# First attention: both kinds of score products issued together over four row groups, output product ahead of the weighing; second mixture: row numbers read behind the third result

## The chip, the core and the metric

One core of one Trainium2 chip runs the whole program in one launch. The time is the device time in microseconds (us) from launch to end; the kernel before has a median of 1166.97 us over 3 runs (1165.14 to 1170.62). The engines named below are TensorE (PE: matrix products; its weight loads are shown as PEld), VectorE (DVE), ScalarE (ACT), GpSimd (POOL) and SyncE (SP), which here only starts DMAs. The engines run side by side, each in its own fixed order, and wait for each other on semaphores that are written out by hand.

## The reference, cut to what matters

Two layers, each an attention and a mixture of experts, over 16 sequences of 128 tokens with 256 features. The change touches the first attention and the last mixture.

```
# first attention: 16 heads of 16, per sequence
qh, kh, vh = split_heads(norm(x) @ Wq + bq), split_heads(ctx @ Wk + bk), split_heads(ctx @ Wv + bv)
attn = softmax(qh @ kh.T / sqrt(16))
x = x + tanh(g) * ((attn @ vh) @ Wo + bo)

# second mixture: 8 experts, each takes its 640 best (token, weight) pairs
kept_w, kept_pair = top_k(where(assigned, pair_w, -inf), 640)
xe = xf[kept_tok]
oe = gelu(xe @ fc1_w.T + fc1_b) @ fc2_w.T + fc2_b
y = zeros.at[kept_tok].add(oe * kept_w)
```

## The kernel before, in words

**First attention (`attention_0`).** A step `t` handles one sequence in several stages at once, a software pipeline over t = -3 to 18; sequence i is normed at step i-3, turned at i-2, projected to queries, keys and values at i-1, scored at i, exponentiated at i+1, weighed with the values at i+2, and multiplied with the output weights at i+3. Beside this, each step turns one half of an expert's weight matrix for the first mixture to signs (18 halves: `below` on POOL, `signs` and `magnitudes` on DVE, `turn_half` on PE, `keep` on ACT); after every odd half the row scales are spread over the partitions (`spread` on PE, then `keep_scale` on ACT, which comes behind `exps(i, 1)` in ACT's order).

The 16 heads sit in four row groups r = 0 to 3 of 32 partitions, four heads in each. Scores are made twice. `scores(i, ph)` makes them with queries as rows (`psS`, 4 products 32 rows deep and 256 columns wide for the row groups 2ph and 2ph+1), only so that DVE can take each row's maximum (`maximum(i, ph)`). `turn_maxima` turns these maxima, ACT copies them, and `less_maxima(i, ph)` makes the scores again with keys as rows (`psT`, 8 products of 32 x 128), and subtracts the maxima with 8 small products of 8 rows (`sel` against `nmT`). ACT then exponentiates `psT` (`exps`), and `weigh` multiplies with the values on PE in four column groups of 32 columns at once. `heads_out` on DVE divides by the sums, `output` on PE multiplies with Wo into one half of the bank `psV`, and `residual` on DVE adds to x. Every fp32 product shows up in a trace as two MATMUL records, so "x8" of `psS` in a timeline is one call of `scores`, and "x16" of `psT` and "x8" of `sel` one call of `less_maxima`.

Both halves ph share two banks of `psS` and two of `psT`. So `scores(i, 1)` waits for `maximum(i, 0)`, and `scores(i+1, 0)` for `maximum(i, 1)` (semaphore `max_done`); likewise `less_maxima` for `exps` (`exp_done`). PE's order in a step: scores(t,0), turn_maxima(t-1), value and project(t+1), less_maxima(t-1,0), scores(t,1), turn_in(t+2), weigh(t-2), turn_half(t), less_maxima(t-1,1), spread(t) if t is odd, output(t-3). DVE's: maximum(t,0), values, normed, maximum(t,1), split, heads_out(t-2), signs, magnitudes, residual(t-3), statistics.

**Second mixture (`feed_forward_1`).** After routing, the tokens are scattered in the order of experts to DRAM (`m_sorted`), with each row's destination in an extra column. Each expert e has 640 rows, NT = 5 tiles of 128. SP loads an expert's rows to `xin[e % 2]` (`load_x`; the name in the trace is `m_turned`), PE turns them, makes the hidden layer (`xup`) and the result (`xdown`), DVE adds the bias into one of NY = 4 buffers (`put`, tile `f_y`), and POOL scatters that buffer to its destinations (`send`, `m_results<-f_y,f_index`). POOL learns the destinations with `read_index(e)`, which waits for the load of `xin[e % 2]`. Expert 0's results are all made before expert 1's tiles are turned (`SECOND`), while the later experts are interleaved (`TURNS`). The fifth result of expert 0 needs the first buffer back, so `put(0, 4)` waits for `send(0, 0)` to land; the turned tiles of expert 1 stand behind it on DVE, and PE waits for those.

Of the kernel before, what the change touches and what calls it, by code (L numbers as in the profile page):

```python
# [138 lines left out]
def attention_0(nc, A, sb, ps, sem, NB, D, KD, x_sb, ctx_sb, ident, gates, x_mean, x_rstd, c_mean, c_rstd,  # L139
# [8 lines left out]
    NG = 4  # L148
    NQK, NV = 3, 4
# [4 lines left out]
    with ExitStack() as c:  # L154
# [7 lines left out]
        sel = sb("a0_sel", [P, NG, P], F32R, c)  # L162
# [54 lines left out]
        def there(i):  # L217
            return 0 <= i < NB

        with nc.Block() as block:  # L220
# [175 lines left out]
            def _(dve):  # L396
# [105 lines left out]
                def step(t):  # L502
# [8 lines left out]
                    if there(t):  # L511
                        maximum(t, 1)
                        split(t)
                    if there(t - 2):
                        heads_out(t - 2)
# [4 lines left out]
                    if there(t - 3):  # L520
                        residual(t - 3)
# [10 lines left out]
            def _(pe):  # L532
# [35 lines left out]
                def scores(i, ph):  # L568
                    b = i % NQK
                    if ph == 0:  # L570
                        pe.wait_ge(s["qk_out"], i + 1)
                    at_least(pe, s["max_done"], 2 * i + ph)
                    for m in range(2):
                        for r in (2 * ph, 2 * ph + 1):
                            ins = pe.matmul(psS[r % 2][:, 2 * m:2 * m + 2, :], q[b][rows(r), m, :], km[b][rows(r), m, :, :],  # L575
                                            start=True, stop=True)
                    ins.then_inc(s["s_done"], 1)
# [6 lines left out]

                def less_maxima(i, ph):
                    b = i % NQK
                    if ph == 0:
                        pe.wait_ge(s["nmc_done"], i + 1)
                    if i == 0:
                        pe.wait_ge(s["sel_done"], 1)  # L590
                    at_least(pe, s["exp_done"], 2 * i + ph)

                    for g in range(NG):
                        for r in (2 * ph, 2 * ph + 1):
                            pe.matmul(psT[r % 2][:, g, :], km[b][rows(r), g // 2, g % 2, :], q[b][rows(r), g // 2, :],
                                      start=(g == 0), stop=False, skip_group_check=True)
                    for g in range(NG):
                        for r in (2 * ph, 2 * ph + 1):
                            ins = pe.matmul(psT[r % 2][:, g, :], sel[32 * r:32 * r + 2 * NG, g, :], nmT[32 * r:32 * r + 2 * NG, :],
                                            start=False, stop=True, skip_group_check=True)  # L600
                    ins.then_inc(s["st_done"], 1)
# [53 lines left out]
                def step(t):  # L655
                    if there(t):
                        scores(t, 0)
# [5 lines left out]
                    if there(t - 1):  # L663
                        less_maxima(t - 1, 0)
                    if there(t):
                        scores(t, 1)
                    if there(t + 2):
                        turn_in(t + 2)
                    if there(t - 2):
                        weigh(t - 2)  # L670
                    if due(t):
                        turn_half(t)
                    if there(t - 1):
                        less_maxima(t - 1, 1)
                    if due(t) and half(t)[1] == 1:
                        spread(t)
                    if there(t - 3):
                        output(t - 3)

                steps(step)  # L680


# [1092 lines left out]
def feed_forward_1(nc, A, sb, ps, sem, NB, NE, CAP, ROW, D, KD, KS, F, x_sb, ctx_sb, ident, gates, xg, yg, m, hT, out):  # L1775
# [8 lines left out]
    with ExitStack() as c:  # L1784
# [90 lines left out]
        with nc.Block() as block:  # L1875
# [227 lines left out]
            def _(pool):  # L2103
# [46 lines left out]
                for e in range(NE):  # L2150
                    if there(e + 2):
                        read_index(e + 2)
                    for t in range(NT):
                        send(e, t)
                        if t % 2 == 0 and done < NB:
                            bias(done)
                            done += 1
# [222 lines left out]
```

## Time and profile before

| | |
|---|---|
| median of 3 runs | 1166.97 us |
| the profiled execution: device time, span | 1168.28 us, 1166.4 us |
| PE busy, PEld busy | 1006.6 us (86%), 923.8 us (79%) |
| DVE, ACT, POOL busy | 792.2, 602.2, 289.0 us |
| first attention, steady steps: stretch 60 to 212 us | PE busy 151.29 of 152 us, DVE 110.00, ACT 95.58 |
| second mixture, first and last `send` issued | 1031.89 and 1146.73 us |
| mean granted PE clock over the span | 0.916 |

The profiled execution is one more run; its 1168.28 us lies 1.3 us above the median of the three. Times in the timelines are microseconds from the start of the span. [...]

### The profile page before, as it was taken

The page shows a single profiled execution, that of the slowest core. Times are in us where ns is not written, and L with a number is a line of the kernel's source. Part 1 is how long each engine was busy: PE and PEld are TensorE (multiplying, and loading weights), DVE is VectorE, ACT ScalarE, POOL GpSimd, SP SyncE. Part 2 cuts the span into 40 slices and gives each one's busy share as a digit, 9 for nine tenths or more (in the row PEclk, how much of TensorE's full clock was granted, in tenths as well). Part 3 has the DMA queues.
Part 4 walks back from the last instruction along what each step waited for, and adds up shares of the span by engine and source line. Part 5 has one row for each costly group of instructions (what it writes and reads, how often), then busy time and mean ns, then how long its engine had stood idle before and what let it go on. Part 6 is the DMA issues. An engine that isn't in the chain of part 4 may idle for free. (4 is left out here: it accounts for less than half of the span.)

```text
span 1166.4 us, 23709 instructions
## 1 busy us (share of the span) xinstructions
PE 1006.6 (86%) x8410; PEld 923.8 (79%) x8410; DVE 792.2 (68%) x1976; ACT 602.2 (52%) x1441; POOL 289.0 (25%) x391
## 2 busy tenths in 40 slices
PE   3899999965889546999999999999939999959993
PEld 2788888755768445999999999999938899859992
DVE  6667676766588596677776777776647876436655
ACT  3365665533578624555555555555523534447660
POOL 3433334213470241100001010010002003725542
PEclk9599999956999877999999999999985999989996
DMA  8321111000243423001010110101001201445417
GB/s 249 112 83 46 49 38 56 2 1 32 72 158 101 100 70 114 31 13 43 1 43 1 44 43 1 43 1 43 1 5 41 70 1 48 145 153 165 140 64 247
DMA packets 74938, 77.91 MB, mean 67 GB/s; under 512 B 19664, under 2 KB 66256, under 8 KB 74448
## 3 DMA queue, kind: packets, MB, share of 16 engines
q1 hardware_dynamic: 68720, 62.33, 17.3%
q0 software_dynamic: 4992, 13.90, 3.4%
q8 instruction: 67, 1.10, 0.4%
q10 hardware_dynamic: 1120, 0.27, 0.1%
q14 instruction: 39, 0.32, 0.1%
HBM read 46.53 MB, written 29.95 MB: 66 GB/s over the span
## 5 line engine op out<-in xcount | busy, mean ns | idle before, releaser
L296 POOL TENSOR_SCALAR t_neg<-t_raw,t_nthr 128x256 bf16<-128x256 f32 (+1 forms) x54 | 60.8, 1141 | 117.1 <-DVE t_nthr L487 117.1
L1600 POOL TENSOR_TENSOR a_toklo<-a_kv,a_tokhi 128x512 fp32r<-128x512 f32 x16 | 22.1, 1379 | 239.6 <-ACT a_tokhi L1542 239.6
L1507 PE MATMUL a_psY<-a_nwhi,a_uhi 128*128 128x256 f32 x256 | 73.4, 287 | 5.0 <-DVE a_ulo L1656 5.0
L1656 DVE TENSOR_TENSOR a_ulo<-a_psU,a_uhi 128x512 fp32r<-128x512 f32 x64 | 44.1, 689 | 42.9 <-ACT a_uhi L1569 42.9
L1628 DVE SCALAR_TENSOR_TENSOR a_klo<-a_psK,a_bk,a_khi 128x512 fp32r<-128x512 f32 x64 | 47.9, 748 | 36.3 <-ACT a_khi L1547 36.3
L1490 PE MATMUL a_psU<-a_pThi,a_toklo 128*128 128x256 f32 x256 | 72.2, 282 | 0.0
L1490 PE MATMUL a_psU<-a_pThi,a_tokhi 128*128 128x256 f32 x256 | 72.2, 282 | 0.0
L1490 PE MATMUL a_psU<-a_pTlo,a_tokhi 128*128 128x256 f32 x256 | 72.1, 282 | 0.0
L1569 ACT ACTIVATE a_uhi<-a_psU 128x512 fp32r<-128x512 f32 x64 | 38.3, 598 | 65.3 <-PE a_psU L1490 65.3
L1507 PE MATMUL a_psY<-a_nwlo,a_uhi 128*128 128x256 f32 x256 | 71.9, 281 | 0.0
L1507 PE MATMUL a_psY<-a_nwhi,a_ulo 128*128 128x256 f32 x256 | 71.9, 281 | 0.0
L1557 ACT ACTIVATE a_probs<-a_psS,a_nmax 128x256 f32<-128x256 f32 x128 | 59.5, 469 | 22.8 <-DVE a_nmax L1638 22.8
L1547 ACT ACTIVATE a_khi<-a_psK,a_bk 128x512 fp32r<-128x512 f32 x64 | 44.0, 688 | 49.9 <-PE a_psK L1450 49.9
L447 DVE TENSOR_REDUCE a_nmax<-a_psS 128x4 f32<-128x512 f32 x64 | 41.0, 681 | 41.7 <-PE a_psS L575 41.7
L1998 PE MATMUL f_psH<-m_turned,m_w 128*128 128x320 f32 x384 | 65.1, 319 | 0.0
L2009 PE MATMUL f_psY<-m_w,f_g_split 128*128 128x256 f32 x480 | 64.5, 286 | 0.0
L2298 DVE TENSOR_TENSOR f_g_split<-f_g,f_g_split 128x320 fp32r<-128x320 f32 x64 | 30.8, 493 | 45.3 <-ACT f_g_split L2068 45.3
L2124 POOL DMA_INDIRECT m_results<-f_y,f_index x40 | 46.3, 1158 | 53.4 <-DVE f_y L2305 51.1
L2009 PEld LDWEIGHTS f_psY<-m_w,f_g_split 128*128 128x128 f32 x480 | 59.5, 188 | 0.0
L1998 PEld LDWEIGHTS f_psH<-m_turned,m_w 128*128 128x128 f32 x384 | 59.2, 196 | 0.0
L1450 PE MATMUL a_psK<-a_kvThi,a_wkhi 128*128 128x512 f32 x128 | 56.9, 444 | 1.9 <-DVE a_kvTlo L1623 1.4
L1551 ACT ACTIVATE a_qhi<-a_psQ,a_bq 128x256 fp32r<-128x256 f32 x64 | 30.3, 474 | 45.4 <-PE a_psQ L1459 45.4
(368 smaller groups left out, 3393.4 us busy)
## 6 DMA issues: line engine op xcount, KB each, us to landing
t_raw<-in_L_ffn_expert_w SPq DMA_DIRECT2D x16, 512.0 KB, 3.7
f_raw<-in_fc_T SPq DMA_DIRECT2D x16, 512.0 KB, 3.9
m_turned<-m_sorted SPq DMA_DIRECT2D x8, 680.0 KB, 5.1
m_sorted<-a_zeros SPq DMA_DIRECT2D x8, 640.0 KB, 3.6
m_results<-a_zeros SPq DMA_DIRECT2D x8, 512.0 KB, 4.9
m_sorted<-m_zeros SPq DMA_DIRECT2D x1, 3072.0 KB, 12.8
e_xin<-m_sorted SPq DMA_DIRECT2D x24, 128.0 KB, 2.2
m_expert_out<-e_y SPq DMA_DIRECT2D x24, 128.0 KB, 1.7
```

The lines of the kernel that those rows point to most:

```text
L296: ins = pool.tensor_scalar(neg[:, own], raw[h % NRAW][:, own], nthr[h % 2][:, n:n + 1], None, ALU.is_lt)
L447: ins = dve.tensor_reduce(nmax[:, r, :], psS[r % 2][:], AX.X, ALU.max, negate=True)
L1450: ins = pe.matmul(psK[:].rearrange("p b t -> p (b t)"), wk[x][:, a, h * DH:(h + 1) * DH], kvT[pair % 2][y][:, a, :, :, :].rearrange("p b m ...
L1490: ins = pe.matmul(psU[b][:, f, :], tok[pair % 2][x][:, b, kt, f * P:(f + 1) * P], pT[gr % 2][y][:, b, kt, :, :].rearrange("p h t -> p (h t)"),
L1507: ins = pe.matmul(psY[:, b, :], u[ch % 2][x][:, f, hh * P:(hh + 1) * P], nw[y][:, f, 2 * j + hh, :], start=first, stop=last, skip_group_ch ...
L1547: act.activation(k_[n % 2][0][:], psK[:], ACT.Identity, bias=bk[:, n % NH:n % NH + 1]).then_inc(s["k_hi"], 1)
L1557: act.activation(probs[n % 2][:, b, :], psS[n % 2][:, b, :], ACT.Exp, bias=nmax[:, n, b:b + 1], accum_out=sums[:, n, b:b + 1]).then_inc(s[ ...
L1628: dve.scalar_tensor_tensor(out=k_[n % 2][1][:], in0=psK[:], scalar=bk[:, n % NH:n % NH + 1], in1=k_[n % 2][0][:].bitcast(F32), op0=ALU.add ...
L1656: dve.tensor_tensor(u[ch % 2][1][:], psU[ch % 2][:], u[ch % 2][0][:].bitcast(F32), ALU.subtract).then_inc(s["u_lo"], 1)
L1998: ins = pe.matmul(psH[k % NG][:, 0:HALF], xw1[e % 2][x][:, a * F + f * P:a * F + (f + 1) * P], xT[e % 2][y_][:, a, rows], start=(n == 0), ...
L2009: ins = pe.matmul(psY[n % 2][:, 0, :], xgs[e % 2][x][:, f, t * P:(t + 1) * P], xw2[e % 2][y_][:, f * D:(f + 1) * D], start=(k == 0), stop= ...
L2124: pool.indirect_dma_start(yg, bass.IndirectOffsetOnAxis(ap=index[e % NI][:, t:t + 1], axis=0), y[n % NY][:], None)\
```

## The change

On PE, `scores` and `less_maxima` become one function. It issues the scores of one sequence for two row groups and the second scores of another sequence for the other two row groups in turn: per m two products of `psS`, then four of `psT`, and at the end the eight small ones. A step now has two such calls, scores(t,1) with less(t-1,0), and scores(t+1,0) with less(t-1,1). Each call first waits for everything that either part needs. `output(t-3)` moves from the end of the step to a place ahead of `weigh(t-2)`, and on DVE `residual(t-3)` moves ahead of `heads_out(t-2)`. On POOL, `read_index(e + 2)` moves from ahead of the first `send` of expert e to behind its third.

```diff
@@ VectorE, step(t) @@
                         maximum(t, 1)
                         split(t)
+                    if there(t - 3):
+                        residual(t - 3)
                     if there(t - 2):
                         heads_out(t - 2)
...
-                    if there(t - 3):
-                        residual(t - 3)
@@ TensorE @@
-                def scores(i, ph):
-                    b = i % NQK
-                    if ph == 0:
+                def scores(i, ph, less, less_ph):
+                    now, then = there(i), there(less)
+                    b, lb = i % NQK, less % NQK
+                    if now and ph == 0:
                         pe.wait_ge(s["qk_out"], i + 1)
-                    at_least(pe, s["max_done"], 2 * i + ph)
+                    if now:
+                        at_least(pe, s["max_done"], 2 * i + ph)
+                    if then and less_ph == 0:
+                        pe.wait_ge(s["nmc_done"], less + 1)
...
+                    if then:
+                        at_least(pe, s["exp_done"], 2 * less + less_ph)
+                    own, other = (2 * ph, 2 * ph + 1), (2 * less_ph, 2 * less_ph + 1)
                     for m in range(2):
-                        for r in (2 * ph, 2 * ph + 1):
+                        for r in own if now else ():
                             ins = pe.matmul(psS[r % 2][:, 2 * m:2 * m + 2, :], q[b][rows(r), m, :], km[b][rows(r), m, :, :],
                                             start=True, stop=True)
+                        for g in (2 * m, 2 * m + 1) if then else ():
+                            for r in other:
+                                pe.matmul(psT[r % 2][:, g, :], km[lb][rows(r), m, g % 2, :], q[lb][rows(r), m, :],
+                                          start=(g == 0), stop=False, skip_group_check=True)
+                    if now:
+                        ins.then_inc(s["s_done"], 1)
+                    for g in range(NG) if then else ():
+                        for r in other:
+                            ins = pe.matmul(psT[r % 2][:, g, :], sel[32 * r:32 * r + 2 * NG, g, :], nmT[32 * r:32 * r + 2 * NG, :],
+                                            start=False, stop=True, skip_group_check=True)
+                    if then:
+                        ins.then_inc(s["st_done"], 1)
@@ TensorE, step(t) @@
-                    if there(t):
-                        scores(t, 0)
                     if there(t - 1):
                         turn_maxima(t - 1)
                     if there(t + 1):
                         value(t + 1)
                         project(t + 1)
-                    if there(t - 1):
-                        less_maxima(t - 1, 0)
-                    if there(t):
-                        scores(t, 1)
+                    scores(t, 1, t - 1, 0)
                     if there(t + 2):
                         turn_in(t + 2)
+                    if there(t - 3):
+                        output(t - 3)
                     if there(t - 2):
                         weigh(t - 2)
                     if due(t):
                         turn_half(t)
-                    if there(t - 1):
-                        less_maxima(t - 1, 1)
+                    scores(t + 1, 0, t - 1, 1)
                     if due(t) and half(t)[1] == 1:
                         spread(t)
-                    if there(t - 3):
-                        output(t - 3)
@@ GpSimd, second mixture @@
                 for e in range(NE):
-                    if there(e + 2):
-                        read_index(e + 2)
                     for t in range(NT):
                         send(e, t)
+                        if t == 2 and there(e + 2):
+                            read_index(e + 2)
```

PE in the steady part of the first attention, from `turn_half` (`a_psQ<-t_identb,t_tern`) of an odd step to the second scores of the next, before:

```order
L640 MATMUL a_psQ<-t_identb,t_tern 128x128 x8
L595 MATMUL a_psT<-a_q,a_km 128x128 x8
L599 MATMUL a_psT<-a_nmT,a_sel 128x128 x8
L649 MATMUL a_psX<-t_diag,m_ones 128x128 x2
L627 MATMUL a_psV<-a_wo,a_oT 128x256 x2
L575 MATMUL a_psS<-a_km,a_q 128x256 x4
L583 MATMUL a_psX<-ident,a_nmw 128x128
L555 MATMUL a_psV<-a_wv,a_xcT 128x256 x2
L564 MATMUL a_psQ<-a_xcT,a_wq 128x128 x4
L564 MATMUL a_psQ<-a_xcT,a_wk 128x128 x4
L595 MATMUL a_psT<-a_q,a_km 128x128 x8
```

The same stretch after the change (here the counts are products, two trace records each where they are fp32):

```order
L645 MATMUL a_psQ<-t_identb,t_tern 128x128 x8
L586 MATMUL a_psS<-a_km,a_q 128x256 x2
L591 MATMUL a_psT<-a_q,a_km 128x128 x4
L586 MATMUL a_psS<-a_km,a_q 128x256 x2
L591 MATMUL a_psT<-a_q,a_km 128x128 x4
L597 MATMUL a_psT<-a_nmT,a_sel 128x128 x8
L654 MATMUL a_psX<-t_diag,m_ones 128x128 x2
L606 MATMUL a_psX<-ident,a_nmw 128x128
L555 MATMUL a_psV<-a_wv,a_xcT 128x256 x2
L564 MATMUL a_psQ<-a_xcT,a_wq 128x128 x4
L564 MATMUL a_psQ<-a_xcT,a_wk 128x128 x4
L586 MATMUL a_psS<-a_km,a_q 128x256 x2
```

The output product and the lone scores no longer stand between the spreading of the scales (`t_diag`) and the turning of the maxima (`a_nmw`), and the first `psT` products of the next step now stand behind two of `psS`.

POOL in the second mixture, from the three reads of row numbers (`f_index`) on, before:

```order
L2118 COPY f_index<-m_turned 128x5 x3
L2124 DMA m_results<-f_y,f_index 9216x256
L2129 TENSOR_TENSOR x_sb<-x_sb,m_b2s 128x256
L2124 DMA m_results<-f_y,f_index 9216x256 x2
L2129 TENSOR_TENSOR x_sb<-x_sb,m_b2s 128x256
```

And after:

```order
L2117 COPY f_index<-m_turned 128x5 x2
L2123 DMA m_results<-f_y,f_index 9216x256
L2128 TENSOR_TENSOR x_sb<-x_sb,m_b2s 128x256
L2123 DMA m_results<-f_y,f_index 9216x256 x2
L2117 COPY f_index<-m_turned 128x5
L2128 TENSOR_TENSOR x_sb<-x_sb,m_b2s 128x256
```

The third read, which waits for the rows of expert 2, stands behind three of expert 0's results instead of ahead of all five.

## Rows read from the trace of the kernel before

**Rows 1.** Windows: stretch, length, busy of PE, PEld, DVE, ACT, POOL, clock, DMA.

```profile
60.00:212.00 152.00, 151.29 (x2151) 126.41 (x2153) 110.00 (x251) 95.58 (x254) 53.21 (x60) 1.00 0.15 48
212.00:217.00 5.00, 5.00 (x82) 4.05 (x83) 2.41 (x6) 2.30 (x6) 2.26 (x3) 0.66 0.00 0
```

**Rows 2.** Timeline of PE, two steady steps: start, length, engine, line, tiles.

```profile
138.99 0.33 PE L583 MATMUL a_psX<-ident,a_nmw 128*128 128x128 f32 x1
...
146.75 0.62 PE L640 MATMUL a_psQ<-t_identb,t_tern 128*128 128x128 bf16 x8
147.30 1.16 PE L595 MATMUL a_psT<-a_q,a_km 32*128 32x128 f32 x16
...
148.78 0.71 PE L649 MATMUL a_psX<-t_diag,m_ones 128*128 128x128 f32 x4
149.33 1.03 PE L627 MATMUL a_psV<-a_wo,a_oT 128*128 128x256 f32 x4
150.29 1.13 PE L575 MATMUL a_psS<-a_km,a_q 32*128 32x256 f32 x8
151.35 0.33 PE L583 MATMUL a_psX<-ident,a_nmw 128*128 128x128 f32 x1
...
154.38 1.16 PE L595 MATMUL a_psT<-a_q,a_km 32*128 32x128 f32 x16
...
155.38 0.48 PE L575 MATMUL a_psS<-a_km,a_q 32*128 32x256 f32 x2
155.43 0.50 PE L599 MATMUL a_psT<-a_nmT,a_sel 8*128 8x128 f32 x6
...
156.45 0.44 PE L545 MATMUL a_psX<-ident,a_xn 128*128 128x128 f32 x2
...
158.92 0.62 PE L640 MATMUL a_psQ<-t_identb,t_tern 128*128 128x128 bf16 x8
...
163.09 0.33 PE L583 MATMUL a_psX<-ident,a_nmw 128*128 128x128 f32 x1
```

**Rows 3.** Timeline of DVE in the same steps.

```profile
146.88 1.76 DVE L461 RECIPROCAL a_rec<-a_psO 128x256 f32<-128x256 f32 x1 [0.79 <-PE a_psO L616]
...
149.01 1.66 DVE L495 SCALAR_TENSOR_TENSOR t_tern<-t_raw,t_thr,t_neg 128x256 bf16<-128x256 f32 x4
...
150.93 0.48 DVE L469 SCALAR_TENSOR_TENSOR x_sb<-a_psV,gates,x_sb 128x256 f32<-128x256 f32 x1
151.33 0.42 DVE L525 BATCH_NORM_STATS2 stats<-ctx_sb 128x6 f32<-128x256 f32 x1
...
151.99 1.27 DVE L447 TENSOR_REDUCE a_nmax<-a_psS 128x4 f32<-128x512 f32 x2
...
161.19 1.40 DVE L495 SCALAR_TENSOR_TENSOR t_tern<-t_raw,t_thr,t_neg 128x512 bf16<-128x512 f32 x2
```

**Rows 4.** Timeline of ACT behind the odd step's `less_maxima`.

```profile
148.89 1.09 ACT L352 ACTIVATE a_pT<-a_psT 128x512 f32<-128x512 f32 x2 [0.47 <-PE a_psT L599]
149.86 0.39 ACT L373 ACTIVATE m_s<-a_psX 128x256 f32<-128x256 f32 x1
```

**Rows 5.** Timeline of PE, the last sequence's scores.

```profile
212.83 1.80 PE L575 MATMUL a_psS<-a_km,a_q 32*128 32x256 f32 x8
```

**Rows 6.** Chain that ended last, second mixture: start, length, what.

```profile
1023.33 7.71 DMA m_turned<-m_sorted
...
1031.16 0.20 POOL f_index L2118
...
1031.89 2.42 DMA m_results<-f_y,f_index
...
1034.41 0.42 DVE f_y L2305
```

**Rows 7.** Timeline of PE behind that chain, with the idle time ahead of it.

```profile
1035.22 1.11 PE L1986 MATMUL f_psX<-ident,m_turned 128*128 128x128 f32 x4 [8.24 <-DVE m_turned L2291]
```

**Rows 8.** Timeline of POOL: the second reading of row numbers.

```profile
1026.41 0.19 POOL L2118 COPY f_index<-m_turned 128x5 uint32<-128x5 uint32 x1 [6.00 <-DMA m_turned<-m_sorted]
```

More of the change, by code:

```diff
@@ L566, in project @@
                     ins.then_inc(s["qk_done"], 1)
-                def scores(i, ph):
-                    b = i % NQK
-                    if ph == 0:
+                def scores(i, ph, less, less_ph):
+                    now, then = there(i), there(less)
+                    b, lb = i % NQK, less % NQK
+                    if now and ph == 0:
                         pe.wait_ge(s["qk_out"], i + 1)
-                    at_least(pe, s["max_done"], 2 * i + ph)
+                    if now:
+                        at_least(pe, s["max_done"], 2 * i + ph)
+                    if then and less_ph == 0:
+                        pe.wait_ge(s["nmc_done"], less + 1)
+                    if less == 0:
+                        pe.wait_ge(s["sel_done"], 1)
+                    if then:
+                        at_least(pe, s["exp_done"], 2 * less + less_ph)
+                    own, other = (2 * ph, 2 * ph + 1), (2 * less_ph, 2 * less_ph + 1)
                     for m in range(2):
-                        for r in (2 * ph, 2 * ph + 1):
+                        for r in own if now else ():
                             ins = pe.matmul(psS[r % 2][:, 2 * m:2 * m + 2, :], q[b][rows(r), m, :], km[b][rows(r), m, :, :],
                                             start=True, stop=True)
-                    ins.then_inc(s["s_done"], 1)
+                        for g in (2 * m, 2 * m + 1) if then else ():
[10 more added lines that the diff above has]
+                        ins.then_inc(s["st_done"], 1)
                 def turn_maxima(i):
@@ L583, in turn_maxima @@
                     pe.transpose(psX[:, 0, :], nmw[:].rearrange("p a b -> p (a b)").bitcast(F32), ident[:]).then_inc(s["nmt_done"], 1)
[L585 to L601, printed above, removed]
                 def weigh(i):
```

## The prediction

> **What bounds the kernel now.** I read the windows first. From 60 to 212 us, the steady part of the first attention, PE is busy 151.29 of 152 us at full clock, DVE 110.00 and ACT 95.58 [rows 1]. So PE sets the time there and what leaves PE can shorten the kernel, until another engine's chain becomes as long. Next the timeline of PE: two steps, one with `spread` and one without, take from 138.99 to 163.09, 24.10 us [rows 2]. [...] Then DVE's and ACT's timelines of the same steps, to see how late each of them hands over what PE's moved calls will want [rows 3, 4]. Last, the chain that ended last in the second mixture: PE stands 8.24 us before its turns [rows 7], and the chain runs from a load of rows over POOL's read of row numbers, a scatter and DVE's `put` to these turns [rows 6].
>
> **First attention, the products alone.** From PE's rows [rows 2]: `less_maxima` by itself takes 147.30 to 148.78, 1.48 us. `scores` by itself takes 150.29 to 151.35, 1.06 us. `less_maxima` followed by `scores` takes 154.38 to 156.45, 2.07 us, already less than the 2.54 of both apart. The reason stands in the same rows: two score records start at 155.38, ahead of six `sel` records that start at 155.43 and stand ahead of them in the program. So the two pairs of row groups do run at once, and a later product overtakes earlier ones in other row groups.
>
> How long is a combined call? The trace shows none. Low bound: the longer of the two, 1.48 us (the chain of 8 fp32 products and the `sel` products of one pair of row groups; the scores need 1.06 and fit beside it). High bound: no more overlap than apart, 2.54 us. I take 1.48, since at 155.38 both pairs of groups ran beside each other. If the combined calls cost that and nobody waited, a step would lose 2.07 - 1.48 = 0.59 us in its first call and 1.06 us in its second, 3.3 us per pair of steps.
>
> **What is late next.** The removed time was also cover. I count from the start W of `turn_half` (146.75 in the odd step), with the order of the change.
>
> - *Odd step, turning the maxima.* `turn_half` 0.55, combined call 1.48, `spread` 0.55 (148.78 to 149.33): PE could turn maxima at W + 2.58. But that writes the bank that `keep_scale` reads, and ACT does `keep_scale` behind `exps`: 148.89, then 149.86 + 0.39 = 150.25, W + 3.50 [rows 4]. Before, output and scores (149.33 to 151.35) covered this. Now PE waits 0.92 + some 0.05 for the semaphore: W + 3.55. Behind it, in PE's order, stand value, projection and everything else. From L583 to the next second scores is 151.35 to 154.38, 3.03 us: W + 6.58.
> - *The first combined call wants `maximum(t+1, 0)`.* Before, only `scores(t, 1)` did, 1 us later and behind `less_maxima`. DVE's chain starts when `weigh` is done (146.88, W + 0.13), runs through reciprocal, signs, magnitudes, residual and statistics and ends with the maximum at 151.99 + 1.27 = 153.26 [rows 3]. The residual (150.93 to 151.33, 0.40) leaves this chain, since it goes ahead of the reciprocal into DVE's wait of 0.79 us there: 152.86, W + 6.11. That is before 6.58, so no wait in the odd step.
> - *Even step.* No `spread`: PE is ready at 0.55 + 1.48 + 3.03 = W + 5.06. DVE's signs come in two instructions instead of four: 1.40 for 1.66 us, so its chain ends at W + 5.85, plus 0.05: PE waits 0.84 us, until W + 5.90.
> - From the first combined call to the next W: 1.48, then turn_in and weigh (156.45 to 158.92) 2.47, then output 0.96 (149.33 to 150.29): 4.91 us.
>
> A step is then 11.49 us from an odd W and 10.81 from an even one, 22.30 for two; before 24.10. That is 1.8 of the possible 3.3 us. Five such pairs lie between the third and the thirteenth turning of maxima: 9.0 us. Moving output ahead of `weigh` costs PE nothing by itself; it makes y ready about 1.9 us before pv, so that DVE's residual fits.
>
> Head: three combined calls stand in steps 0 to 2, where PE is partly at half clock and where one waits for a maximum that comes late anyway. Between nothing and 2 us; I take 1.0 us gained. Tail: step 15 has no projection, so PE comes to its combined call some 2.8 us earlier than in a normal step and waits for DVE's maximum; the products of `less_maxima(14, 0)`, which fill that time before, now wait with it. The last scores start at 212.83 before and take 1.80 us at the lower clock [rows 5]; now 1.48 and the output (0.96) stand between the maximum and `weigh`, and `spread` is followed by the same wait of 0.97. I take 2 us lost (bounds: nothing, and 4 if the clock drops twice). The first attention gains 9.0 + 1.0 - 2.0 = 8.0 us. All that follows it starts when it ends.
>
> **Second mixture.** POOL's third read waits for expert 2's rows, whose load takes from 1023.33 for 7.71 us, to 1031.04. Then 1031.16 read, 1031.89 scatter of result 0, 2.42 us to landing, 1034.41 `put(0, 4)`, and 1035.22 PE [rows 6, 7]. The second read is done at 1026.41 + 0.19 [rows 8], and results 0 to 3 are ready by then. So the first scatter goes out 1031.16 - 1026.41 = 4.75 us earlier, at 1027.14. It lands after 2.42 us if undisturbed (gain 4.75); but expert 2's rows are just being loaded until 1031.04, and in the worst case its packets come out behind all of these and it lands no earlier than before (gain 0). I take a landing shortly behind the load's end, 1031.5: a gain of 2.8 us. The third read then waits for nothing new, and later ones stand a few us behind where they stood; the loads that ask for them are issued an expert ahead, so I cost that at nothing. Were this cover gone, PE would wait for rows at the next expert.
>
> **Sum.** 8.0 + 2.8 = 10.8 us from the profiled execution's 1168.28: 1157.5. Against the median of 1166.97 it is 1156.2. I forecast 1157 us.
>
> **Rivals.**
>
> *A, strict order.* The products may start strictly in program order, with overlap only at the seams. By [rows 2] a `psT` record takes 1.48 less the `sel` part, about 0.91 over 8 in a group, 0.11 us; a `psS` record 0.22. In a combined call each m then is one score record followed by four `psT` records, 0.22 + 0.45, and the second m overlaps by one: 1.2 + 0.57 for `sel` = 1.8 us. Three of the four calls of a pair are on the path (the fourth lies under the 0.84 us of the even step): 3 x 0.31 x 5 = 4.7 us, and 1 at the ends. 1163 us. Against it stands 155.38 before 155.43. [...] Chance 0.13.
>
> *B, slower: four row groups don't add up.* If the groups share a stream or a write port so that a combined call takes 2.54 us, each costs 1.06 more. Per pair 3 x 1.06 + (1.06 - 0.84) = 3.4 us, x 5 = 17, and 3 at the ends: 1177 us. The balance turns where a combined call exceeds about 2.1 us. For it: only the small `sel` products (8 rows) are seen beside scores, never two full fp32 streams. Against it: `weigh` runs four column groups at once. Chance 0.06.
>
> *C, slower by the clock.* PE had no waits in the steady steps; now one of 0.8 to 1.0 us in each. In the tail, a short wait amid products on two row groups was enough for a stretch with granted clock 0.66, in which 1.06 us of scores took 1.80 [rows 1, 5], some 1.7 us lost over the stretch. Once per step, 13 times: 22 us, 1179 us; from about six such stretches on the gain is gone. Against it: combined calls fill the array better than what they replace, and each wait has about 3 us of full-array products on one side. Chance 0.07.
>
> *D, only the attention gains.* The scatter is held up by the load: 1160 us. Chance 0.12.
>
> *E, the waits don't bind.* If a chain is shorter than I read it, up to 3.3 us a pair come through: 1157 - 7.5, about 1149 us. Chance 0.07.
>
> My forecast has 0.55. What this measurement can tell from no change is about 0.5%, 5.8 us: below 1161.1 is faster. From the forecast, 0.5 of its 0.55 fall there; with D (0.08) and E (0.07) that is 0.65. Within 0.5%: 0.05 + 0.04 + 0.13 of A, 0.22. Slower: B and C, 0.13. The range 1149 to 1168 leaves out B, C and a little at the low end.
>
> **What would show it.** In the timeline of PE after the change: a combined call of 1.5 us from its first record to the next full-array record (2.1 and more: B; 1.8: A); a wait of about 0.95 us before the turning of maxima behind each `spread`, released by ACT's copy to `m_s`; a wait of about 0.85 us for `a_nmax` before the combined call of every other step; two steps in 22.3 us; granted clock 1.00 in the steady part. In the second mixture, the first scatter about 4.7 us after the second read instead of behind the third, with an idle time of PE before expert 1's second turns of about 5.5 us instead of 8.24. The prediction is wrong if the waits are absent, if two steps take more than 23.5 us, or if PE's clock falls there.

## The result, and the profile after

The changed kernel takes 1159.14 us (median of 7 runs, 1155.98 to 1160.02), the kernel before 1166.97 beside it (7 runs, 1165.14 to 1171.27). The medians lie 7.8 us apart; the ratio, taken over all runs, is 0.9921, 95% interval 0.9899 to 0.9942, which is about 9 us faster. The forecast was 1157. The profiled execution of the changed kernel took 1155.98 us with a span of 1154.2; before 1168.28 and 1166.4.

The windows come first, over the steady part and over the tail of the first attention (columns as in [rows 1]).

```profile
60.00:195.00 135.00, 123.98 (x2036) 109.70 (x2033) 105.12 (x241) 90.81 (x240) 51.62 (x58) 1.00 0.17 52
195.00:223.00 28.00, 22.51 (x341) 18.50 (x341) 16.66 (x35) 9.92 (x20) 7.43 (x8) 0.82 0.01 1
```

PE was busy 151.29 of 152 us in [rows 1]; now it is busy 92% of the steady part, still at full clock. It waits for something there, and in the tail its mean clock is 0.82. The timeline of PE says what it waits for. This is a pair of steady steps; it answers to [rows 2].

```profile
125.81 0.62 PE L645 MATMUL a_psQ<-t_identb,t_tern 128*128 128x128 bf16 x8
126.36 0.48 PE L586 MATMUL a_psS<-a_km,a_q 32*128 32x256 f32 x2
126.37 0.49 PE L591 MATMUL a_psT<-a_q,a_km 32*128 32x128 f32 x4
...
127.28 0.64 PE L597 MATMUL a_psT<-a_nmT,a_sel 8*128 8x128 f32 x8
127.86 0.33 PE L606 MATMUL a_psX<-ident,a_nmw 128*128 128x128 f32 x1
...
131.73 0.48 PE L586 MATMUL a_psS<-a_km,a_q 32*128 32x256 f32 x2 [0.89 <-DVE a_nmax L447]
...
136.57 0.62 PE L645 MATMUL a_psQ<-t_identb,t_tern 128*128 128x128 bf16 x8
...
138.62 0.71 PE L654 MATMUL a_psX<-t_diag,m_ones 128*128 128x128 f32 x4
140.24 0.30 PE L606 MATMUL a_psX<-ident,a_nmw 128*128 128x128 f32 x1 [0.90 <-ACT m_s L373]
...
148.02 0.62 PE L645 MATMUL a_psQ<-t_identb,t_tern 128*128 128x128 bf16 x8
```

Records overlap here (the 0.62 us of L645 from 125.81 reach past the next start at 126.36), so a group's cost is taken from its first start to the first start of the next group. A combined call runs from 126.36 to 127.86, 1.50 us: L586 (the scores for the maxima, `psS`) and L591 (the scores for the softmax, `psT`) start 0.01 us apart, on two pairs of row groups. Behind `spread` (L654) the turning of the maxima (L606) waits 0.90 us for ACT; in the step without `spread` the combined call waits 0.89 us for DVE's maximum. From one `turn_half` (L645) to the next it is 10.76 and 11.45 us, 22.21 for two, where [rows 2] have 24.10.

DVE's timeline shows the chain behind the 0.89, answering to [rows 3].

```profile
125.94 1.76 DVE L461 RECIPROCAL a_rec<-a_psO 128x256 f32<-128x256 f32 x1 [1.43 <-PE a_psO L621]
...
129.74 0.42 DVE L525 BATCH_NORM_STATS2 stats<-ctx_sb 128x6 f32<-128x256 f32 x1
130.08 0.41 DVE L474 BATCH_NORM_STATS2 stats<-x_sb 128x6 f32<-128x256 f32 x1
130.40 1.27 DVE L447 TENSOR_REDUCE a_nmax<-a_psS 128x4 f32<-128x512 f32 x2
...
134.80 0.48 DVE L469 SCALAR_TENSOR_TENSOR x_sb<-a_psV,gates,x_sb 128x256 f32<-128x256 f32 x1 [0.18 <-PE a_psV L632]
```

The maximum ends at 131.67 and PE starts at 131.73. The residual (L469) now lies ahead of the reciprocal, in a wait that DVE has anyway. Two statistics stand ahead of the maximum and belong to other row blocks; the experiments use this. ACT, answering to [rows 4]:

```profile
138.73 1.09 ACT L352 ACTIVATE a_pT<-a_psT 128x512 f32<-128x512 f32 x2 [0.48 <-PE a_psT L597]
139.70 0.39 ACT L373 ACTIVATE m_s<-a_psX 128x256 f32<-128x256 f32 x1
```

PE's last steps of the first attention, answering to [rows 5]:

```profile
194.10 0.33 PE L606 MATMUL a_psX<-ident,a_nmw 128*128 128x128 f32 x1
...
197.97 0.80 PE L586 MATMUL a_psS<-a_km,a_q 32*128 32x256 f32 x2 [3.54 <-DVE a_nmax L447]
...
200.74 2.07 PE L632 MATMUL a_psV<-a_wo,a_oT 128*128 128x256 f32 x4
...
208.90 0.30 PE L606 MATMUL a_psX<-ident,a_nmw 128*128 128x128 f32 x1 [0.90 <-ACT m_s L373]
...
211.15 2.08 PE L632 MATMUL a_psV<-a_wo,a_oT 128*128 128x256 f32 x4
```

PE waits 3.54 us, and right behind that the output product takes 2.07 us where it takes 1.03 in a steady step. The granted clock is 0.50 from 197.22 to 204.05 and from 210.88 to 214.29, 10.2 us in all; before it was 0.50 for 3.4 us.

The second mixture: the chain that ended last, then POOL and PE, answering to [rows 6], [rows 8] and [rows 7].

```profile
1012.54 4.42 DMA m_turned<-m_sorted
...
1017.09 0.20 POOL f_index L2117
...
1017.83 4.26 DMA m_results<-f_y,f_index
...
1022.18 0.42 DVE f_y L2304
```
```profile
1017.09 0.19 POOL L2117 COPY f_index<-m_turned 128x5 uint32<-128x5 uint32 x1 [5.92 <-DMA m_turned<-m_sorted]
1017.83 0.98 POOL L2123 DMA_INDIRECT m_results<-f_y,f_index  x1 [0.54 <-POOL f_index L2117]
...
1021.99 0.20 POOL L2117 COPY f_index<-m_turned 128x5 uint32<-128x5 uint32 x1
```
```profile
1022.99 1.12 PE L1985 MATMUL f_psX<-ident,m_turned 128*128 128x128 f32 x4 [5.33 <-DVE m_turned L2290]
```

The first scatter (L2123) goes out behind the second read of row numbers and not behind the third. It takes 4.26 us to land beside the load of rows, where it took 2.42 in [rows 6]. The load of expert 2's rows lands at 1021.75 us and the scatter at 1022.09, 0.34 us behind it. The kernels e1 and e2 below repeat this: in e1 the scatter goes out behind that load and takes 2.42 us; in e2 it goes out during the load, takes 4.26 us and lands 0.36 us behind it. PE waits 5.33 us in place of 8.24.

A budget by stretches, from the starts of single instructions. "End" is the start of the last but one of the first attention's statistics of `x` (the last one starts 1.77 us later before and 1.83 after), "put" is DVE's `put` (L2304 of the changed kernel).

| stretch | before | after | gained | forecast |
|---|---|---|---|---|
| start to first turning of maxima | 34.79 | 32.37 | 2.42 | - |
| 1st to 4th turning (head) | 44.29 | 41.23 | 3.06 | 1.0 |
| 4th to 14th turning (five pairs) | 120.46 | 111.06 | 9.40 | 9.0 |
| 14th turning to end (tail) | 33.51 | 38.54 | -5.0 | -2.0 |
| put(0,3) to put(0,4) | 11.46 | 8.51 | 2.95 | 2.8 |

Without the first row this is 10.4 us, against 10.8 in the forecast's sum. The 2.42 us of the first row are not the change's: e2 below has the old attention and needs 32.55 us there. The head scatters too. In four profiled runs with the changed kernel's head (after, e1, c_after, e8) it takes 41.23 to 42.90 us, the shorter ones with 10.2 us at a granted clock of 0.50 and the longer ones with 17.1.

### The profile page after: what moved, and what is told of

Its sections match the earlier page's. It is cut to its first block and busy times, and to the rows that moved or that the text cites. A ratio compares the mean times of both kernels' runs of the same rounds, so it can differ in the third digit from the quotient of the medians.

```text
span 1154.2 us, 23709 instructions
## 1 busy us (share of the span) xinstructions
PE 980.9 (85%) x8410; PEld 911.9 (79%) x8410; DVE 792.4 (69%) x1976; ACT 602.2 (52%) x1441; POOL 284.5 (25%) x391
## 5 line engine op out<-in xcount | busy, mean ns | idle before, releaser
L2123 POOL DMA_INDIRECT m_results<-f_y,f_index x40 | 42.1, 1053 | 61.0 <-DVE f_y L2304 58.6
L586 PE MATMUL a_psS<-a_km,a_q 32*128 32x256 f32 x256 | 39.4, 429 | 19.3 <-DVE a_nmax L447 17.8
```

Of the source, the lines that this page charges most:

```text
L2123: pool.indirect_dma_start(yg, bass.IndirectOffsetOnAxis(ap=index[e % NI][:, t:t + 1], axis=0), y[n % NY][:], None)\
```

## Experiments

Ratios are to the kernel before, run in the same group on the same chip. "Pair" is two steady steps, "ten" the stretch from the 4th to the 14th turning, "tail" as in the budget. The first four ran on one chip, e11 on another. The group of c_after, e5 to e10 ran on a third one, where the kernel before took 1202 us; what differs there lies outside the attention, as the last section shows.

| kernel | us (lowest to highest) | ratio, 95% interval | pair | ten | tail |
|---|---|---|---|---|---|
| e1_attention_only | 1160.11 (1158.08 to 1162.21) | 0.9928 [0.9907, 0.9948] | 22.21 | 111.06 | 38.42 |
| e2_index_only | 1165.70 (1162.80 to 1169.97) | 0.9981 [0.9965, 0.9998] | 24.10 | 120.46 | 31.89 |
| e3_old_places | 1157.64 (1156.41 to 1159.51) | 0.9909 [0.9890, 0.9929] | 22.95 | 114.76 | 35.65 |
| e4_grouped | 1159.96 (1158.95 to 1161.94) | 0.9930 [0.9911, 0.9950] | 22.25 | 111.27 | 39.84 |
| c_after | 1194.60 (1190.86 to 1196.42) | 0.9926 [0.9905, 0.9947] | 22.21 | 111.06 | 38.53 |
| e5_spread_first | 1188.89 (1188.13 to 1193.37) | 0.9893 [0.9871, 0.9915] | 21.79 | 108.91 | 39.30 |
| e6_stats_late | 1191.60 (1190.67 to 1195.95) | 0.9906 [0.9885, 0.9927] | 21.56 | 107.79 | 38.33 |
| e7_both | 1180.07 (1176.84 to 1185.26) | 0.9812 [0.9786, 0.9838] | 20.48 | 102.38 | 36.37 |
| e8_tail_apart | 1194.71 (1189.88 to 1196.66) | 0.9938 [0.9919, 0.9958] | 22.21 | 111.06 | 38.25 |
| e9_all | 1179.93 (1177.77 to 1182.29) | 0.9818 [0.9798, 0.9837] | 20.48 | 102.39 | 35.88 |
| e10_residual_back | 1227.44 (1225.29 to 1230.86) | 1.0216 [1.0195, 1.0238] | 27.21 | 136.06 | 47.91 |
| e11_apart | 1166.20 (1164.07 to 1168.43) | 0.9995 [0.9982, 1.0008] | 23.18 | 115.93 | 40.36 |

The texts on record call the products into `psS` those of the magnitudes, the products into `psT` score blocks of the softmax, and a sequence a row block. They have one slip, from c_after on: they give the step without `spread` ("even") 11.45 us and the one with it ("odd") 10.76. It is the other way round, as the prediction had it. The waits are named rightly.

**Each half of the change by itself.** e1 undoes the move of `read_index`:

```
+                    if there(e + 2):
+                        read_index(e + 2)
                     for t in range(NT):
                         send(e, t)
-                        if t == 2 and there(e + 2):
-                            read_index(e + 2)
```

> The change without its second part: the third reading of row numbers stands ahead of expert 0's first result again. If the two parts add, this loses the 3.0 us that the profiles show between expert 0's fourth and fifth result, and nothing else: some 3 us above the changed kernel, some 6 to 7 us below the kernel before. In the trace: fifth result 15.4 us behind the fourth is gone to 11.5 us (before: 1022.95 to 1034.41) instead of 8.5. Rival: the loads and turns of later experts hide it, and the time is that of the changed kernel.

e2 is the kernel before with only that move.

> Only the second part: row numbers read behind the third result, the first attention as before. If the parts add: 3 us below the kernel before, about 1164 us, and a first attention with two steps in 24.1 us. Rival: same as before, within 1 us.

Between put(0,3) and put(0,4) e1 has 11.47 us and e2 8.51, as before and after have them. The attention is the larger part and the row numbers a small one, 0.2% by ratio, with an interval that ends just below 1; the parts add up within the intervals. The two share a chip, so they also price head and tail: 45.43 and 42.62 us in the head (2.8 gained), 31.89 and 38.42 in the tail (6.5 lost).

**The places undone, the combined calls kept.**

```
                         turn_in(t + 2)
-                    if there(t - 3):
-                        output(t - 3)
                     if there(t - 2):
                         weigh(t - 2)
...
                         spread(t)
+                    if there(t - 3):
+                        output(t - 3)
```

and DVE's `residual(t - 3)` goes back behind `magnitudes(t + 2)`.

> The combined score calls as in the changed kernel, but the output product stays at the end of PE's step and the residual behind the magnitudes on DVE, as before. Theory one: output then covers ACT's copy of the scales (the wait of 0.90 us ahead of the turning of maxima goes), but the residual is late on DVE, at W + 4.0 to 4.6, and value(t+1) waits for it, so that two steps take 22.7 us against 22.2 in the changed kernel: some 3 us slower than the changed kernel. Theory two: only the two waits seen in the changed kernel count, the cover helps and nothing new is late: two steps in 20.8 us, some 9 us faster than the changed kernel.

The timeline of PE has a new wait in each step in place of the two known ones:

```profile
130.99 1.10 PE L555 MATMUL a_psV<-a_wv,a_xcT 128*128 128x256 f32 x4 [1.27 <-DVE x_sb L469]
...
142.59 1.10 PE L555 MATMUL a_psV<-a_wv,a_xcT 128*128 128x256 f32 x4 [0.84 <-DVE x_sb L469]
```

The value product waits for the residual, which reads the other half of the same tile, and the residual is late at its old place. Two steps take 22.95 us (expected 22.7). So in the steady part the new places are worth 3.7 us over ten steps. The whole kernel is still not slower than the changed one: its tail is 2.9 us shorter, with one stretch of 6.8 us at a granted clock of 0.50 where the changed kernel has 10.2 us. This part of the expectation failed.

**All score products first.** One loop becomes two, so that four score products stand ahead of the eight others in the program:

```
                                             start=True, stop=True)
-
+                    for m in range(2):
                         for g in (2 * m, 2 * m + 1) if then else ():
```

> In a combined call all four score products of psS are issued first, then all eight of psT, then the eight small ones; the changed kernel issues them in turn, 2, 4, 2, 4, 8. If later products overtake earlier ones in other row groups, a combined call stays at 1.5 to 1.6 us and the time is that of the changed kernel within 1.5 us. If products start strictly in program order, with overlap only at the seams, psT would start behind the last psS: about 0.65 + 0.9 + 0.57 = 2.1 us a call, two steps in 24 us, some 10 us slower than the changed kernel.

```profile
128.30 0.48 PE L586 MATMUL a_psS<-a_km,a_q 32*128 32x256 f32 x2
128.33 0.49 PE L591 MATMUL a_psT<-a_q,a_km 32*128 32x128 f32 x4
...
128.62 0.38 PE L586 MATMUL a_psS<-a_km,a_q 32*128 32x256 f32 x2
...
129.82 0.33 PE L606 MATMUL a_psX<-ident,a_nmw 128*128 128x128 f32 x1
```

The call takes 1.52 us, and the products into `psT` start 0.03 us behind the first scores, although six more score records stand ahead of them in the program, which start at 128.62 and later. Rival A, strict order, falls.

**The combined calls undone, the places kept.**

```
-                    scores(t, 1, t - 1, 0)
+                    scores(NB, 1, t - 1, 0)
+                    scores(t, 1, NB, 0)
...
-                    scores(t + 1, 0, t - 1, 1)
+                    scores(NB, 0, t - 1, 1)
+                    scores(t + 1, 0, NB, 1)
```

`NB` stands for "none": each call does one of the two jobs.

> Edit: all places of the changed kernel are kept (output product ahead of the weighing, residual ahead of the heads, row numbers behind the third result), but each combined call is taken apart again: first the score blocks of the softmax with two row groups, behind them the magnitudes' products with the other two. Theory one (the saving is the combined call's, 2.54 - 1.50 = 1.04 us a call, and the places only let it through): TensorE's work of two steps, 22.21 - 0.90 - 0.89 = 20.42 us, grows by four times 1.04 to 24.6, and both waits disappear behind it: two steps 24.1 to 24.6 us, 120.5 to 123 us over ten steps, the kernel level with the kernel before or up to 0.3% slower. Rival (the new places save time by themselves, 0.74 us in two steps as between the old-places kernel and the changed one): two steps 23.4 us, 117 us over ten, 3 us faster than the kernel before.

```profile
127.50 1.16 PE L591 MATMUL a_psT<-a_q,a_km 32*128 32x128 f32 x16
128.41 0.31 PE L597 MATMUL a_psT<-a_nmT,a_sel 8*128 8x128 f32 x2
128.51 0.48 PE L586 MATMUL a_psS<-a_km,a_q 32*128 32x256 f32 x2
128.56 0.50 PE L597 MATMUL a_psT<-a_nmT,a_sel 8*128 8x128 f32 x6
128.83 0.81 PE L586 MATMUL a_psS<-a_km,a_q 32*128 32x256 f32 x6
```

Expected by the first theory were 120.5 to 123 us over ten steps, and by the rival 117; measured 115.93. The mistake is to be seen in these rows: the scores begin at 128.51, beside the `sel` products. Standing next to each other already gives part of the overlap, 2.07 us for the two jobs as [rows 2] had it, and not 2.54. With 2.07 the pair is 20.42 + 4 x 0.57 = 22.7 us, and with the wait of 0.57 for ACT that remains 23.3; measured 23.18. So the four kernels before (120.46), places alone (115.93), combined calls alone (114.76) and both (111.06) make a table: 4.5 and 5.7 us by each alone, 9.4 by both. What the places save can be read from the rows only in part. They bring the second pair of jobs of each step side by side, 2.54 - 2.07 = 0.47 us a step and 0.94 of work a pair, where 0.92 is gained. But the wait of 0.57 is new, so some 0.5 us come from elsewhere on PE, which was not taken apart. Over the whole kernel e11 gains nothing: its tail takes 40.36 us, with the clock at 0.50 for 13.6 us of it.

**The output early, the residual late.** Only the residual's move is undone.

> Edit: the output product stays ahead of the weighing, VectorE's adding of the residual goes back behind the maximum of the next magnitudes' place that it had before. Theory one (what the moved places bring in the steady steps comes from TensorE not waiting at the row turning and from VectorE's order): even steps about 0.4 us longer than in the changed kernel, odd ones the same, 2 to 2.5 us slower over the ten steady steps. Rival (the residual's place is free, the output product's place is all that counts): steps 22.21 us for two, 0 us.

It is 32.8 us slower than c_after, against the 2 to 2.5 expected; both theories fail. First DVE, then PE, then windows of PE (columns as in [rows 1]).

```profile
124.63 1.76 DVE L461 RECIPROCAL a_rec<-a_psO 128x256 f32<-128x256 f32 x1 [2.09 <-PE a_psO L621]
...
128.69 0.48 DVE L469 SCALAR_TENSOR_TENSOR x_sb<-a_psV,gates,x_sb 128x256 f32<-128x256 f32 x1
```
```profile
128.16 0.30 PE L606 MATMUL a_psX<-ident,a_nmw 128*128 128x128 f32 x1 [0.90 <-ACT m_s L373]
129.31 1.70 PE L555 MATMUL a_psV<-a_wv,a_xcT 128*128 128x256 f32 x4 [0.85 <-DVE x_sb L469]
130.81 1.91 PE L564 MATMUL a_psQ<-a_xcT,a_wq 128*128 128x128 f32 x8
...
143.17 1.90 PE L555 MATMUL a_psV<-a_wv,a_xcT 128*128 128x256 f32 x4 [2.18 <-DVE x_sb L469]
```
```profile
119.44:129.68 10.24, 8.49 (x154) 7.19 (x153) 6.62 (x16) 7.36 (x18) 0.80 (x1) 1.00 0.02 6
129.68:133.09 3.41, 3.41 (x15) 3.13 (x14) 2.41 (x6) 0.00 (x0) 3.41 (x5) 0.50 0.42 148
```

By the program's order and the releasers in these rows a ring is closed: value product, projections, combined call, output product and weighing in PE's order, then reciprocal, signs, magnitudes and residual in DVE's, then the next value product. The output product (0.96 us in [rows 2]) is now inside it. And behind the waits PE's clock falls to 0.50 for 3.4 us in eight of the ten steady steps; the queries' products take 1.91 us in place of 1.05. This is rival C of the prediction, seen in the steady part, though not in the changed kernel. No run takes the ring and the clock apart, but the ten steps allow an estimate. Of the five with `spread`, two had no fall and take 12.47 us each, the three others 13.98 to 14.12. That is some 1.6 us a fall, so of the 25.0 us lost over ten steps some 13 are the clock's and some 12 the ring's. e3 has the same late residual with the output product outside the ring: its step with `spread` takes 11.61 us, 0.86 less than the 12.47 here.

**The two waits.** e5 moves `spread` ahead of the second combined call, and on ACT `keep_scale` ahead of `exps(t - 1, 1)`:

```
                         turn_half(t)
-                    scores(t + 1, 0, t - 1, 1)
                     if due(t) and half(t)[1] == 1:
                         spread(t)
+                    scores(t + 1, 0, t - 1, 1)
```

e6 moves the two statistics of DVE behind `values(t + 1)` of the next step; e7 does both. c_after is the changed kernel as their comparison.

```
                         values(t + 1)
+                    if there(t - 2):
+                        dve.bn_stats(c_stats[:, t - 2, :], ctx_sb[:, t - 2, :])
+                    if there(t - 4):
+                        statistics(t - 4)
...
-                    if there(t - 1):
-                        dve.bn_stats(c_stats[:, t - 1, :], ctx_sb[:, t - 1, :])
-                    if there(t - 3):
-                        statistics(t - 3)
```

> The changed kernel again, unaltered, as the comparison of this group. Both theories: 1157 to 1160 us, 0.992 of the kernel before; two steady steps 22.21 us (10.76 odd, 11.45 even).

> Edit: behind a spread, TensorE's spread product stands ahead of the second combined call and ScalarE keeps the scale ahead of the exponentials of the second half. Theory one (a steady odd step is set by the wait of 0.90 us of the turning of the maxima for ScalarE's keeping of the scale, and VectorE is only about 0.45 us less late): the wait of 0.90 goes, a wait of about 0.45 for VectorE's maximum of magnitudes takes its place, the odd step falls from 10.76 to about 10.3 us, the kernel is 3 to 4 us faster than the changed kernel. Rival (the 0.90 is slack that something else takes up at once): steps unchanged, 0 us.

> Edit: VectorE's statistics of the next attention rows and of the finished row block are issued behind the maximum of the next magnitudes in place of ahead of it. Theory one (an even step is set by VectorE's maximum being late by 0.89 us): the even step falls from 11.45 to about 10.8 us, the odd one keeps its 0.90 us of wait for the scale, the kernel is 4 to 5 us faster than the changed kernel. Rival (VectorE is full, so that moving its work only moves the wait to another product): steps unchanged, 0 us.

> Both edits, of the spread ahead and of the late statistics. Theory one: each kind of step had one wait, and VectorE's 0.45 us that showed behind the removed 0.90 is gone too, so odd falls by 0.90 and even by 0.66: two steps about 20.65 against 22.21 us, 9 to 11 us faster than the changed kernel, more than the two edits alone add up to. Rival (VectorE is full): no more than the first edit alone brings, 0 to 4 us.

The combined call of the step with `spread` in e5, then both waits of e6:

```profile
141.15 0.48 PE L586 MATMUL a_psS<-a_km,a_q 32*128 32x256 f32 x2 [0.65 <-DVE a_nmax L447]
```
```profile
131.61 0.48 PE L587 MATMUL a_psS<-a_km,a_q 32*128 32x256 f32 x2 [0.24 <-DVE a_nmax L447]
...
140.12 0.30 PE L607 MATMUL a_psX<-ident,a_nmw 128*128 128x128 f32 x1 [0.90 <-ACT m_s L373]
```

In e5 the wait for ACT is gone and one of 0.65 for DVE stands in its place: the step goes from 11.45 to 11.02 us. In e6 the other step goes from 10.76 to 10.11 and the wait for ACT stays. In e7 it is 10.11 and 10.36, and one wait of 0.24 is left per pair. Over ten steps the gains are 2.2, 3.3 and 8.7 us: both together bring more than the sum, because the statistics also stood behind the 0.65. So the two waits were on the path, each with the engine named. The whole kernels are 5.7, 3.0 and 14.5 us under c_after, where 3 to 4, 4 to 5 and 9 to 11 were expected; runs of one kernel lie 5 to 8 us apart on this chip, so the ten steps are the better measure. At 0.9812 of the kernel before, e7 is, with e9 below, the fastest of this study. In the profiled runs of c_after and e7 8.7 us of the difference are in the ten steps, 2.1 in the head and 2.2 in the tail.

**The last step.** Only for the last row block the two jobs are issued apart, the ready one first.

```
-                    scores(t, 1, t - 1, 0)
+                    if t == NB - 1:
+                        scores(NB, 1, t - 1, 0)
+                        scores(t, 1, NB, 0)
+                    else:
+                        scores(t, 1, t - 1, 0)
```

> Edit: only in the last step, the score blocks of the softmax of row block 14 are issued by themselves ahead of the wait for the maximum of the magnitudes, and the magnitudes of row block 15 (second half) behind it, instead of as one combined call. Theory one (the tail lost 5.0 us because TensorE stood 3.54 us behind VectorE's maximum and its clock was at its lower level for 10.2 us there against 3.4 us before): the wait is partly filled with some 1.5 us of products that block 14's exponentials wait for, and the stretch from the turning of the maxima of step 13 to the last statistics of the attention falls from 38.5 to between 35.5 and 38.1 us; steady steps unchanged at 22.21. Rival (the clock alone decides the tail, and issuing apart doubles the score products' time): 0 to 1 us slower.

> The spread ahead, the late statistics, and the last step's blocks issued apart, all three. Theory one: two steady steps 20.48 us as with the first two edits alone, the tail 0 to 2 us shorter than theirs (36.4 us), so 0.979 to 0.981 of the kernel before. Rival (with the two edits the last step's wait is only 2.9 us or less and the clock pattern differs, so the third edit is worth nothing or loses the overlap): 0 to 1 us slower than the two edits alone, 0.981 to 0.982.

```profile
195.60 1.16 PE L591 MATMUL a_psT<-a_q,a_km 32*128 32x128 f32 x16 [1.09 <-ACT a_nmT L345]
...
198.05 2.08 PE L586 MATMUL a_psS<-a_km,a_q 32*128 32x256 f32 x8 [0.90 <-DVE a_nmax L447]
200.06 2.08 PE L632 MATMUL a_psV<-a_wo,a_oT 128*128 128x256 f32 x4
```

The wait of 3.54 us is broken up into 1.09 and 0.90, but the clock still falls (to 0.50 from 197.41), the scores take 2.08 us, and the tail is 0.3 us shorter, less than the 0.4 that was the least expected. Both whole-kernel results are the same as without the edit within their intervals. The edit is worth nothing that can be measured.

## Why the prediction was right

- *Combined call, 1.48 us:* measured 1.50 to 1.52. The overtaking read from 155.38 ahead of 155.43 in [rows 2] is real; e4 shows it for full products.
- *Waits of 0.97 and 0.84 us:* measured 0.90 and 0.89, by the engines named. The 0.05 us that stand in them for the semaphore measure 0.06 from DVE's maximum (131.67) to PE (131.73). e5 to e7 take them away, but for 0.24 us, and the time goes with them. Steps 11.49 and 10.81: measured 11.45 and 10.76.
- *The saving in its parts:* the prediction priced the second call at 1.06 us saved by the overlap as a whole. e11 shows that about half of the steady gain (4.5 of 9.4 us) is to be had by the new places alone.
- *The residual's move:* taken as one that shortens DVE's chain by 0.40 us. e10 shows that it carries the whole: without it the early output product closes a ring. It cost nothing to the forecast, since the change holds both.
- *Head, 1.0 us gained:* about 3 (2.8 between e2 and e1), past the upper bound of 2 in both pairs, though one and the same head varies by 1.7 us between runs. Why it gains more was not taken apart.
- *Tail, 2.0 us lost:* the mis-sized term, 5.0 here and 6.5 between e2 and e1, past the bound of 4 that was given for a clock that drops twice. The wait was foreseen and measures 3.54 us. What was too small is the clock's part, at 0.50 for 10.2 us. The attention of e2 and of the kernel before is one and the same program, 31.89 us in the tail at full clock throughout and 33.51 with one stretch of 3.4 us at 0.50: 1.6 us a stretch. The changed kernel has 6.8 us more of it, which by this pair is some 3.2 of the 5.0; the rest, some 1.8, is the wait and the order, as an estimate.
- *Second mixture, 2.8 us:* 2.95. The assumed landing, 4.36 us behind the issue, measures 4.35 to the `put` (1017.83 to 1022.18). The forecast took the scatter to land shortly behind the load's end, 0.46 us; it is 0.34.
- *Sum:* head and tail miss in opposite directions, +2 and -3. The median came out 2.1 us above the forecast. That it came so near is luck as far as head and tail go; the 9.0 us of the steady steps and the 2.8 of the second mixture are not, since waits and steps came as read. e1 at 0.9928 confirms the larger part. The smaller one stands firm in e2's trace (3.0 us), while e2's time (0.9981, interval to 0.9998) only just shows it.
- *Rivals:* A and B fall by e4 and the 1.50 us; the four column groups named against B do run at once before (`weigh` starts 64 records in 1.89 us from 157.03, 0.03 us each, the queries' projection 8 of the same width in 0.89, 0.11 each). C does not occur in the steady steps, but by the estimates above it is some 3 of the 5 us that the tail lost and about half of what e10 lost. C took one short wait in the tail (0.37 us at 211.37 before) as enough for a fall; in e2, the same attention, the same wait at 210.27 was followed by none. That a fuller array holds the clock up, as C's chance assumes, was the author's estimate and is shown by no run. D falls by the gap between the two `put`s (8.51 us, and 11.47 in e1); E's reserve exists, but had to be freed by e7.

## What to carry to other kernels

When one engine is full, compute for each product that is moved or shortened what it hid: here nearly half of a possible 3.3 us a pair turned into two waits. Reordering other engines afterwards removed one and cut the other from 0.89 to 0.24 us, together for more than the sum of each alone. Products on different row groups overlapped here as soon as they stood side by side in the program (2.07 us for jobs of 1.48 and 1.06), so ask first what adjacency alone brings. A reordering that puts a product ahead of another can close a ring through a shared bank, as in e10 (25.0 us lost over ten steps, some 12 of them by the ring, as an estimate): follow who frees the bank before moving only one end.

## What the runs showed that was not expected

- *What came before each fall of the clock.* In the steady part one wait of 0.9 us in a step did not lower it (1.00 in the window). In e10's ten steps it fell at each of the five waits of 2.18 us, but at the waits of 0.90 and 0.85 us close to each other only three times of five (not at 101.85 and 183.81). In the tail it fell with 3.54 us of idle time, again behind waits of 0.90 and 0.37, and in e8 also where the same stretch held two waits of 1.09 and 0.90. So the waits alone do not tell whether it falls. What a fall costs shows where the program is the same: some 1.6 us in the tail (e2 and the kernel before), and 1.5 to 1.65 in a step of e10.
- *A chip on which PE stands for no recorded reason.* In the group of c_after, the waits of PE from 990 to 1030 us (us in all, times, longest), and one product there:

```profile
PE f_psH L1942 <- issue: 26.1, 18, 3.1
```
```profile
1019.76 0.37 PE L1942 MATMUL f_psH<-m_turned,m_w 128*128 128x256 f32 x1 [2.43 <-issue]
```

  No engine or transfer is recorded as releasing them. PE is busy 13.66 of these 40 us. The products of this line run from 901.8 to 1027.9 us there, 126 us, and from 890.0 to 983.0 in the changed kernel on the first chip, 93 us; these 33 us are most of the 35 that lie between the two medians. put(0,4) then follows put(0,3) by 1.44 us in every kernel profiled there: the wait that the move of the row numbers shortens is hidden. The steady steps are the same to 0.01 us, so the comparisons of the attention hold. In these 40 us the DMA records have POOL's scattering of rows and a load of them, and no transfer of the two queues that the page lists as `instruction` (q8 and q14); what holds PE back stays open.
